# One mixing stage: two vector steps moved to GpSimd, value sums joined, the block solve's products spread over four column groups, and new turn orders

## The chip, the core and the metric

The program runs on one core of a Trainium2 chip. Five engines work side by side and meet only at semaphores: PE (TensorE, matrix products; PEld is its weight loading), DVE (VectorE), ACT (ScalarE), POOL (GpSimd) and SP (SyncE, which here only issues DMAs). The metric is the device time of one execution in microseconds (us), a median over several runs.

## The reference, cut to what matters

The program is one decoder layer on x of shape 32 x 128 x 256 (float32): a delta-rule attention, a cross attention and a mixture of experts, each followed by a layer norm. The change lies in the last part of the first of them, which for each head (H = 4, 64 values wide) and each row computes:

```python
T = inv(eye(32) - attn)                    # per chunk of 32 rows
u_i = u0 - w_i @ S ; o_i = q_i @ S + local @ u_i      # the delta rule, chunk by chunk
paths = stack([fir3(v), fir15(v), fir64(v), delta_path, v], axis=3)      # 5 paths of 64 per head
stats = mean, mean of squares, mean of |.|, norm of every path
logits = gelu(concat([hs, stats]) @ gW1 + gb1) @ gW2 + gb2
probs = softmax(logits / tau) * keep + eps
o = sum over paths of probs * paths
o = o * rsqrt(mean(o * o) + 1e-5) * norm_w
x = layernorm(x + o @ Wo)
```

The kernel solves the delta rule of a sequence of 128 rows as a triangular system of four blocks of 32 rows: each block's rows are a product of a matrix (`solver_blocks`) with the right side, in which the blocks solved before have been put in place.

## The kernel before

Everything happens in `mix_paths`. It works on pairs of sequences (P = 2, 16 pairs), 128 rows on the partitions. `staged_pair_loop` gives every engine a list of steps with a lag: in turn n of that engine's list, a step with lag k handles pair n - k. The list is the engine's program order, and an engine executes strictly in that order; between engines only the semaphores count. The first turns and the last ones are written out, the middle is a loop of two turns. A turn is one pass through a list.

What the steps do (lines of the kernel before):

- **PE**: `solve_rows(c)` (L1067), c = 0 to 3, forms block c of the solution: 8 products (2 sequences x 4 heads), each 128 rows x 32 columns of weights and 64 moving columns, all of one c into the same 32 PSUM partitions `rows` = 32c to 32c + 31, side by side in 512 columns. It waits for the block before to be copied back (`row_kept`). `scores` (L1033) makes the causal scores, `delta_rows` (L1079) the delta path, `cross_blocks` (L1047) the cross terms of the next pair, `hidden_x(0..3)` (L1103) and `hidden_stats(0..1)` (L1116) the gate's hidden layer, `logits` (L1126) its output, `statsT` (L1086) turns the statistics, `mixedT` (L1138) and `output` (L1146) turn the mix and multiply it by Wo.
- **ACT**: `keep_rows(c)` (L1183) copies block c from PSUM into `beta_r_v_to_solution`, one 32 x 512 copy, same partitions out as in. `keep_cross` (L1171, three copies), `norms` (L1199, a square root), `copy_stats` (L1206), `gelu(0..1)` (L1217), `exps` (L1226), `square_delta` (L1161), `square_paths` (L1191, L1193), `square_mix` (L1233), `copy_mixed` (L1240), `normalize` (L1246). Each of square root, gelu and exp is preceded by an ACT_TABLE_LOAD.
- **DVE**: `path_sums(t)` (L1289 over the filtered paths, L1290 over the values, sum and absolute sum for each of two sequences), `delta_sums` (L1297), `square_sums` (L1304), `mask_scores` (L1265), `shift_logits` (L1311 to L1321), `probabilities` (L1327 to L1337), `scale_delta` (L1276), `sum_paths` (L1347, and L1352 that adds the weighted delta path), `mix_norm` (L1357, L1360), `scale_mix` (L1366), `residual` (L1372 to L1385), `ln_shift` (L1392).
- **POOL**: `make_rhs` (L1411), `weight` (L1431, L1434), and two inverse roots, `mix_inverse` (L1441) and `ln_inverse` (L1449).
- **SP**: `load_solver`, `load_keys`, `load_gate`, `load_x`, `load_grams`, each waiting until its buffer's readers are done.

Waits that matter below: `cross_blocks` of a pair waits for `shift_logits` (semaphore `shifted`) of the pair two before it, since both use one PSUM bank; `scale_delta` waits until the pair two before it has had its delta path added (`mix_summed`), since both use one buffer; `square_mix` writes `residual`, which `normalize` of the pair before reads, so it waits for `x1_done`; `mix_norm` waits for `square_mix`.

## Time and profile before

| | us |
|---|---|
| median of 3 runs | 1570.22 |
| lowest and highest | 1565.67, 1572.8 |
| the profiled execution's own time | 1569.91 |
| its span, first to last instruction | 1568.2 |
| busy: PE, DVE, ACT, POOL | 1355.5, 915.1, 689.8, 541.7 |
| `mix_paths`, in that span | about 319 to 672 |

All sums below are made against the profiled execution (1569.91 us, of which 1568.2 is the span); the median lies 0.3 us above it. Of the rest of the program nothing is changed, so only the stretch of `mix_paths` is read: who is busy in a turn, who waits for whom, and how far apart the turns are. A row of the timeline merges like instructions: its start, its length to the end of the last of them, engine, line, names, shapes, count. Two neighbours on one engine often overlap by some 0.08 us, so what an instruction costs its engine is the distance to the next start, called its pace here. One product of float32 operands is recorded as two MATMULs, so 8 products are x16.

### The profile page before, as it was taken

Reading aid. Unit: us, or ns where it says so; the run is one execution under the profiler, and the core shown is the slowest. Engines: PE = TensorE matmul, PEld = TensorE weight load, DVE = VectorE, ACT = ScalarE, POOL = GpSimd, SP = SyncE. Lnnn points to the kernel's source line nnn. Section 1 sums busy time; section 2 is a strip of 40 time slices with the busy share of each in tenths; the row PEclk is TensorE's granted clock in tenths of the full one; section 3 lists DMA queues with packets and bytes.
Section 4 is the critical chain, followed back from the end, with each engine's and each line's share of the span. In section 5 each row is a group of like instructions: output and inputs, shape, how many; then the busy total and the mean of one; then the engine's idle time right before and its main releaser. Section 6 shows DMA issues by size and latency. Waiting matters only on the chain. (4 is left out here: it accounts for less than half of the span.)

```text
span 1568.2 us, 24828 instructions
## 1 busy us (share of the span) xinstructions
PE 1355.5 (86%) x8188; PEld 1035.6 (66%) x8189; DVE 915.1 (58%) x1735; ACT 689.8 (44%) x1253; POOL 541.7 (35%) x460
## 2 busy tenths in 40 slices
PE   4889556669999999569999999969979999999995
PEld 1344456658888888358888888855756666666653
DVE  4899759769999999535454445446512212122196
ACT  2545349947777777323433343331022222222214
POOL 2565500014555555522312331211234444444311
PEclk9999878889999999679999999979989999999998
DMA  3698787744333332042232021023021111111164
GB/s 89 149 244 234 207 221 198 216 121 104 95 94 94 94 94 61 14 123 71 85 98 98 31 62 61 28 81 110 0 74 54 57 57 55 56 56 57 59 200 134
DMA packets 147325, 158.20 MB, mean 101 GB/s; under 512 B 63440, under 2 KB 112176, under 8 KB 145712
## 3 DMA queue, kind: packets, MB, share of 16 engines
q1 hardware_dynamic: 134320, 123.63, 27.0%
q0 software_dynamic: 8320, 29.37, 7.3%
q10 hardware_dynamic: 4608, 4.20, 0.8%
q8 instruction: 46, 0.75, 0.2%
q14 instruction: 31, 0.25, 0.1%
HBM read 104.72 MB, written 42.99 MB: 94 GB/s over the span
## 5 line engine op out<-in xcount | busy, mean ns | idle before, releaser
L2531 DVE TENSOR_TENSOR hidden<-unit_psum,gate 128x352 f32<-128x352 f32 x72 | 37.8, 525 | 210.1 <-ACT gate L2494 210.1
L1944 POOL TENSOR_TENSOR scores<-scores,score_max 128x1024 f32<-128x1024 f32 x32 | 60.8, 1899 | 243.2 <-DVE score_max L1872 243.2
L478 PE MATMUL proj_psum<-filtered 128*128 128x512 f32 x192 | 96.0, 648 | 34.8 <-DMA filtered<-in_xT 28.1
L2462 PE MATMUL unit_psum<-wd,hiddenT 128*128 (+1 forms) x432 | 112.0, 395 | 14.2 <-issue 12.9
L549 PE MATMUL proj_psum<-window,toep 128*128 128x128 f32 x512 | 77.2, 319 | 46.8 <-DMA toep<-in_fir 24.3
L2393 POOL DMA_INDIRECT unit_rows<-x_rows,token_of_slot x72 | 69.8, 970 | 126.9 <-PE unit_psum L2436 104.4
L668 ACT ACTIVATE filtered<-proj_psum 32x512 f32<-32x512 f32 x168 | 98.6, 587 | 30.3 <-PE proj_psum L549 26.3
L549 PEld LDWEIGHTS proj_psum<-window,toep 128*128 128x128 f32 x512 | 73.4, 231 | 50.5 <-issue 47.6
L697 DVE SCALAR_TENSOR_TENSOR filtered<-proj_psum,conv_taps,filtered 128x508 f32<-128x508 f32 (+1 forms) x144 | 95.0, 733 | 19.3 <-ACT filtered L596 19.3
L2400 POOL DMA_INDIRECT outs<-unit_out,choice_of_slot x72 | 71.1, 987 | 99.8 <-DVE unit_out L2536 97.1
L2462 PEld LDWEIGHTS unit_psum<-wd,hiddenT 128*128 128x128 f32 (+1 forms) x432 | 76.4, 190 | 37.0 <-issue 29.1
L2445 PE MATMUL unit_psum<-wg,rowsT 128*128 x288 | 98.5, 465 | 0.6 <-ACT rowsT L2488 0.6
L2445 PE MATMUL unit_psum<-wu,rowsT 128*128 x288 | 98.1, 464 | 0.0
L2494 ACT ACTIVATE gate<-unit_psum 128x352 f32<-128x352 f32 x72 | 33.4, 463 | 132.1 <-PE unit_psum L2445 132.1
L478 PEld LDWEIGHTS proj_psum<-filtered 128*128 128x128 f32 x192 | 37.8, 207 | 77.9 <-issue 70.2
L2500 ACT ACTIVATE hiddenT<-unit_psum 128x256 f32<-128x256 f32 x72 | 27.6, 383 | 112.6 <-PE unit_psum L2453 112.6
L2445 PEld LDWEIGHTS unit_psum<-wu,rowsT 128*128 128x128 f32 x288 | 55.3, 192 | 31.1 <-issue 1.0
L1067 PEld LDWEIGHTS mix_psum<-beta_r_v_to_solution,solver_blocks 128*32 128x32 f32 x1024 | 59.4, 111 | 21.9 <-issue 16.0
L1067 PE MATMUL mix_psum<-beta_r_v_to_solution,solver_blocks 128*32 128x64 f32 x1024 | 69.7, 222 | 1.4 <-ACT beta_r_v_to_solution L1183 1.4
L2536 DVE COPY unit_out<-unit_psum 128x256 f32<-128x256 f32 x72 | 30.6, 424 | 67.6 <-PE unit_psum L2462 66.6
L1103 PE MATMUL mix_psum<-xT_tiles,gate_w_x 128*128 128x256 f32 x256 | 66.3, 392 | 0.0
L831 POOL TENSOR_TENSOR qk_ssq<-qk_ssq,minus_half 128x32 f32<-128x32 f32 x8 | 43.5, 5437 | 54.3 <-DVE qk_ssq L711 54.3
(286 smaller groups left out, 3258.5 us busy)
## 6 DMA issues: line engine op xcount, KB each, us to landing
toep<-in_fir SPq DMA_DIRECT2D x32, 384.0 KB, 4.0
neg_decay_blocks<-in_gw1s POOLq DMA_DIRECT2D x8, 1280.0 KB, 10.6
ndg<-filtered SPq DMA_DIRECT2D x8, 1024.0 KB, 6.1
neg_decay_gram<-ndg SPq DMA_DIRECT2D x16, 512.0 KB, 3.7
ctxT_tiles<-in_ctxT SPq DMA_DIRECT2D x16, 512.0 KB, 3.6
gathered<-outs SPq DMA_DIRECT2D x32, 256.0 KB, 3.0
window<-value SPq DMA_DIRECT2D x32, 192.0 KB, 4.0
filtered<-in_xT SPq DMA_DIRECT2D x8, 512.0 KB, 7.0
```

Source lines behind the costliest of these rows:

```text
L478: mm = pe.matmul(psum[:, pair_bank(n, p, m % 2), :], wqkv[m // KD][:, k, (m % KD) * 128:(m % KD) * 128 + 128], xT[:, u, k, :], start=(k == ...
L549: mm = pe.matmul(fir_psum[:, half_of(n), TC * w + c, :], toep[:, w, c, :], window[:, u, :, TC * w + c, :], start=True, stop=True)
L668: act.activation(out, kept, ACT.Copy).then_inc(kept_act[half_of(n)], 1)
L697: ins = dve.scalar_tensor_tensor(out=acc[:, :, s:L], in0=raw[:, :, 0:L - s], scalar=taps[:, c // KD, c % KD, TAPS - 1 - s:TAPS - s], in1=a ...
L831: pool.tensor_tensor(ssq[:, u, :, :], ssq[:, u, :, :], wide(wide(M.minus_half[:, 0], [128, 2 * H], 1), [128, BB, 2 * H], 1), ALU.pow).then ...
L1067: mm = pe.matmul(psum[rows, SOLVE, at:at + DV], solver[:, u, t, h, rows], xs[:, u, at:at + DV], start=True, stop=True)
L1103: mm = pe.matmul(psum[:, GATE + m // 2, at:at + P * L], gw1x[:, k, m * 128:m * 128 + 128], xT[:, k, :], start=(m % 2 == 0 and k == 0), sto ...
L1944: pool.tensor_tensor(sc[:, i % 2, t, :, :], sc[:, i % 2, t, :, :], wide(mx[:, t, :], [128, XH, L], 2), ALU.subtract).then_inc(shifted[t], 1)
L2393: pool.indirect_dma_start(out=rows[:, u, :], out_offset=None, in_=M.x2_dram[:, :], in_offset=bass.IndirectOffsetOnAxis(ap=M.token_of[:, n: ...
L2400: pool.indirect_dma_start(out=M.outs_dram[:, :], out_offset=bass.IndirectOffsetOnAxis(ap=M.choice_of[:, n:n + 1], axis=0), in_=done[:, u, ...
L2445: mm = pe.matmul(psum[:, u, bank, 0:EH], rowsT[:, u, k, :], w[:, bass.ds(chosen["gate_up"], 1), k, :].rearrange("p e n -> p (e n)"), start ...
L2462: mm = pe.matmul(psum[:, u, DOWN, 0:D], hidT[0:HR[t], u, t, :], M.wd[0:HR[t], bass.ds(chosen["down"], 1), t, :].rearrange("p e n -> p (e n)"),
```

## The change

1. `solve_rows(c)`: product (t, h) goes to PSUM partitions 32h to 32h + 31 (column group h of the array) and columns 64t on, instead of partitions 32c on and columns 256t + 64h on. `keep_rows(c)` becomes four copies of 32 x 128, one for each head, from partitions 32h on to partitions 32c on.
2. `path_sums` handles both sequences in one step: the value reductions are joined, 2 of 128 x 512 instead of 4 of 128 x 256. The 4 reductions over the filtered paths stay.
3. The addition of the delta path (`add_delta`) and `scale_mix` are issued by POOL instead of DVE.
4. All five lists have a new order, some lags are changed (POOL's `weight` 2 to 3, ACT's `exps` 1 to 2, SP's `load_x` 3 to 4), and two semaphores are added.

```diff
@@ sync @@
-            staged_pair_loop(sp, PAIRS, (load_solver, 1), (load_keys, 1), (load_gate, 1), (load_x, 3), (load_grams, 0))
+            staged_pair_loop(sp, PAIRS, (load_solver, 1), (load_x, 4), (load_keys, 1), (load_grams, 0), (load_gate, 1))
@@ tensor, solve_rows @@
-                            mm = pe.matmul(psum[rows, SOLVE, at:at + DV], solver[:, u, t, h, rows], xs[:, u, at:at + DV],
-                                           start=True, stop=True)
+                            mm = pe.matmul(psum[h * CB:h * CB + CB, SOLVE, t * DV:t * DV + DV], solver[:, u, t, h, rows],
+                                           xs[:, u, at:at + DV], start=True, stop=True)
@@ tensor, statsT @@
+                pe.wait_ge(path_sums_made, i + 1)
+                pe.wait_ge(delta_sums_made, i + 1)
@@ tensor @@
-            staged_pair_loop(pe, PAIRS, (solve_rows(0), 1), (hidden_x(2), 2), (hidden_x(3), 2), (solve_rows(1), 1),
-                             (mixedT, 4), (output, 4), (statsT, 2), (scores, 1), (hidden_stats(0), 2), (solve_rows(2), 1),
-                             (hidden_stats(1), 2), (solve_rows(3), 1), (logits, 2), (hidden_x(0), 1), (delta_rows, 1),
-                             (cross_blocks, 0), (hidden_x(1), 1))
+            staged_pair_loop(pe, PAIRS, (solve_rows(0), 1), (scores, 1), (hidden_x(0), 2), (hidden_x(2), 2),
+                             (solve_rows(1), 1), (hidden_x(3), 2), (mixedT, 4), (hidden_x(1), 2), (statsT, 2), (solve_rows(2), 1),
+                             (output, 4), (hidden_stats(0), 2), (hidden_stats(1), 2), (solve_rows(3), 1), (logits, 2), (delta_rows, 1),
+                             (cross_blocks, 0))
@@ scalar, keep_rows @@
-                    act.activation(xs[rows, u, :], psum[rows, SOLVE, :], ACT.Copy).then_inc(row_kept, 1)
+                    for h in range(H):
+                        a = act.activation(xs[rows, u, :].rearrange("p (b h d) -> p b h d", b=P, h=H)[:, :, h, :],
+                                           psum[h * CB:h * CB + CB, SOLVE, 0:P * DV].rearrange("p (b d) -> p b d", b=P), ACT.Copy)
+                    a.then_inc(row_kept, 1)
@@ scalar @@
-            staged_pair_loop(act, PAIRS, (square_delta, 1), (keep_cross, 0), (keep_rows(0), 0), (copy_mixed, 3), (norms, 1),
-                             (keep_rows(1), 0), (copy_stats, 1), (gelu(0), 1), (keep_rows(2), 0), (gelu(1), 1),
-                             (keep_rows(3), 0), (normalize, 3), (square_mix, 2), (exps, 1), (square_paths, 0))
+            staged_pair_loop(act, PAIRS, (exps, 2), (square_delta, 1), (keep_cross, 0), (keep_rows(0), 0), (norms, 1),
+                             (keep_rows(1), 0), (copy_mixed, 3), (copy_stats, 1), (keep_rows(2), 0), (gelu(0), 1), (gelu(1), 1),
+                             (keep_rows(3), 0), (square_paths, 0), (normalize, 3), (square_mix, 2))
@@ vector, path_sums @@
-                    for s, mag in ((0, False), (2, True)):
-                        dve.tensor_reduce(stat[:, u, t, 0:12, s], fir, AX.XY, ALU.add, apply_absolute_value=mag)
-                        dve.tensor_reduce(stat[:, u, t, 16:20, s], val, AX.XY, ALU.add, apply_absolute_value=mag)
+                for s, mag in ((0, False), (2, True)):
+                    for t in range(P):
+                        ins = dve.tensor_reduce(stat[:, u, t, 0:12, s], filtered_heads(M, tile(j, u, t)), AX.XY, ALU.add,
+                                                apply_absolute_value=mag)
+                    ins = dve.tensor_reduce(stat[:, u, :, 16:20, s], val, AX.X, ALU.add, apply_absolute_value=mag)
+                ins.then_inc(path_sums_made, 1)
@@ vector @@
-            staged_pair_loop(dve, PAIRS, (residual, 4), (sum_paths, 3), (ln_shift, 4), (mask_scores, 1), (path_sums(1), 0),
-                             (shift_logits, 2), (mix_norm, 3), (probabilities, 2), (scale_delta, 1), (scale_mix, 3),
-                             (delta_sums, 1), (square_sums, 1), (path_sums(0), 0))
+            staged_pair_loop(dve, PAIRS, (mask_scores, 1), (residual, 4), (sum_paths, 3), (ln_shift, 4),
+                             (shift_logits, 2), (scale_delta, 1), (mix_norm, 3), (delta_sums, 1), (probabilities, 2), (square_sums, 1),
+                             (path_sums, 0))
@@ gpsimd @@
+            def add_delta(j, u):
+                i = 2 * j + u
+                pool.wait_ge(mix_step, i + 1)
+                pool.tensor_tensor(mixed[:, :, :], mixed[:, :, :], delta[:, u, :, :], ALU.add).then_inc(mix_summed, 1)
+            def scale_mix(j, u):
+                i = 2 * j + u
+                pool.wait_ge(mix_power, i + 1)
+                own = mixed[:, :, :].rearrange("p b (h d) -> p (b h) d", d=DV)
+                pool.tensor_tensor(own, own, wide(mix_r[:, :], [128, P * H, DV], 2), ALU.mult).then_inc(mix_scaled, 1)
-            staged_pair_loop(pool, PAIRS, (ln_inverse, 4), (make_rhs, 0), (mix_inverse, 3), (weight, 2))
+            staged_pair_loop(pool, PAIRS, (make_rhs, 0), (weight, 3), (ln_inverse, 4), (add_delta, 3), (mix_inverse, 3),
+                             (scale_mix, 3))
```

The order of instructions at the places that the prediction speaks of, before and after. `path_squares` is written by the squaring steps, `value` by `normalize`, `residual<-mixed` by `square_mix`, `gate_exps` by `exps`, `gate_hiddenT` by `gelu`. ACT before, from the two gelus to the squares of the next pair:

```order
L1217 ACTIVATE gate_hiddenT<-mix_psum,gb 128x256 x2
L1183 ACTIVATE beta_r_v_to_solution<-mix_psum 32x512
L1217 ACTIVATE gate_hiddenT<-mix_psum,gb 128x256 x2
L1183 ACTIVATE beta_r_v_to_solution<-mix_psum 32x512
L1246 ACTIVATE value<-residual,ln_shift,ln_inverse_std 128x256 x2
L1233 ACTIVATE residual<-mixed 128x512
L1226 ACT_TABLE_LOAD
L1226 ACTIVATE gate_exps<-gate_logits 128x2x4x5
L1191 ACTIVATE path_squares<-filtered 128x768 x2
L1193 ACTIVATE path_squares<-value 128x2x256
```

ACT after, from the same gelus:

```order
L1224 ACTIVATE gate_hiddenT<-mix_psum,gb 128x256 x4
L1188 ACTIVATE beta_r_v_to_solution<-mix_psum 32x2x64 x4
L1198 ACTIVATE path_squares<-filtered 128x768 x2
L1200 ACTIVATE path_squares<-value 128x2x256
L1253 ACTIVATE value<-residual,ln_shift,ln_inverse_std 128x256 x2
L1240 ACTIVATE residual<-mixed 128x512
```

The squares of the paths now stand ahead of `normalize`, `exps` opens the next turn, and each copy of a block is four.

PE before, from `solve_rows(0)` on (32x64 is a product of the solve; the operand names are printed in the order moving, weights or the reverse):

```order
L1067 MATMUL mix_psum<-beta_r_v_to_solution,solver_blocks 32x64 x8
L1103 MATMUL mix_psum<-xT_tiles,gate_w_x 128x256 x4
L1067 MATMUL mix_psum<-beta_r_v_to_solution,solver_blocks 32x64 x8
L1138 MATMUL mix_psum<-ident,mixed 128x128 x4
L1146 MATMUL mix_psum<-wo,mixedT 128x256 x4
L1086 MATMUL mix_psum<-ident,path_stats 80x128 x2
L1033 MATMUL mix_psum<-qT_tiles,kT_tiles 128x128 x8
L1116 MATMUL mix_psum<-path_statsT,gw1s 128x256 x2
L1067 MATMUL mix_psum<-beta_r_v_to_solution,solver_blocks 32x64 x8
```

PE after, from `solve_rows(0)` on:

```order
L1069 MATMUL mix_psum<-beta_r_v_to_solution,solver_blocks 32x64 x8
L1035 MATMUL mix_psum<-qT_tiles,kT_tiles 128x128 x8
L1107 MATMUL mix_psum<-xT_tiles,gate_w_x 128x256 x4
L1069 MATMUL mix_psum<-beta_r_v_to_solution,solver_blocks 32x64 x8
L1107 MATMUL mix_psum<-xT_tiles,gate_w_x 128x256 x2
L1142 MATMUL mix_psum<-ident,mixed 128x128 x4
L1107 MATMUL mix_psum<-xT_tiles,gate_w_x 128x256 x2
L1090 MATMUL mix_psum<-ident,path_stats 80x128 x2
L1069 MATMUL mix_psum<-beta_r_v_to_solution,solver_blocks 32x64 x8
L1150 MATMUL mix_psum<-wo,mixedT 128x256 x4
L1120 MATMUL mix_psum<-path_statsT,gw1s 128x256 x4
```

Between `mixedT` and `output` there are now three other steps, and `output` stands ahead of the gate's second part, behind `solve_rows(2)`.

DVE after, from `sum_paths` to the sums of the delta path:

```order
L1355 TENSOR_REDUCE mixed<-filtered 128x256 x2
L1392 SCALAR_TENSOR_TENSOR ln_shift<-ln_mean_var,ln_inverse_std 128x2
L1319 TENSOR_TENSOR gate_logits<-mix_psum,gb 128x40
L1323 TENSOR_TENSOR gate_logits<-gate_logits,inv_tau 128x40
L1327 TENSOR_REDUCE gate_sums<-gate_logits 128x8
L1329 TENSOR_TENSOR gate_logits<-gate_logits,gate_sums 128x40
L1283 TENSOR_TENSOR delta_path<-mix_psum,rq 128x512
L1363 TENSOR_REDUCE mixed_mean_squares<-residual 128x8
L1366 TENSOR_SCALAR mixed_mean_squares<-mixed_mean_squares 128x8
L1304 TENSOR_REDUCE path_stats<-delta_path 128x2x4 x2
```

Before, `mask_scores` and four sums of `path_sums` stood between `ln_shift` and `shift_logits`; now they stand ahead of `residual`.

## Rows read from the trace of the kernel before

**Rows 1.** DVE timeline, starts of `square_sums`: start us, length us, engine, line, operation, names, shapes, count
```profile
341.59 2.81 DVE L1304 TENSOR_REDUCE path_stats<-path_squares 128x40 f32<-128x2560 f32 x1
...
396.15 2.81 DVE L1304 TENSOR_REDUCE path_stats<-path_squares 128x40 f32<-128x2560 f32 x1
...
612.59 2.80 DVE L1304 TENSOR_REDUCE path_stats<-path_squares 128x40 f32<-128x2560 f32 x1
```

**Rows 2.** DVE timeline, one turn in the middle of the stage
```profile
478.50 0.58 DVE L1290 TENSOR_REDUCE path_stats<-value 128x4 f32 x1
...
482.34 1.98 DVE L1347 TENSOR_REDUCE mixed<-filtered 128x256 f32 x2
...
485.01 0.15 DVE L1392 SCALAR_TENSOR_TENSOR ln_shift<-ln_mean_var,ln_inverse_std 128x2 f32<-128x2 f32 x1
...
488.93 0.18 DVE L1311 TENSOR_TENSOR gate_logits<-mix_psum,gb 128x40 f32<-128x40 f32 x1
...
489.62 0.20 DVE L1321 TENSOR_TENSOR gate_logits<-gate_logits,gate_sums 128x40 f32<-128x40 f32 x1
...
492.36 1.09 DVE L1366 TENSOR_TENSOR mixed<-mixed,mixed_inverse_norms 128x512 f32<-128x512 f32 x1
493.38 1.27 DVE L1297 TENSOR_REDUCE path_stats<-delta_path 128x8 f32<-128x512 f32 x2
```

**Rows 3.** PE timeline, one turn in the middle of the stage
```profile
473.71 1.99 PE L1103 MATMUL mix_psum<-xT_tiles,gate_w_x 128*128 128x256 f32 x8
475.63 1.08 PE L1067 MATMUL mix_psum<-beta_r_v_to_solution,solver_blocks 128*32 128x64 f32 x16
476.64 0.66 PE L1138 MATMUL mix_psum<-ident,mixed 128*128 128x128 f32 x4
478.06 1.99 PE L1146 MATMUL mix_psum<-wo,mixedT 128*128 128x256 f32 x8 [0.76 <-ACT mixedT L1240]
479.89 0.38 PE L1086 MATMUL mix_psum<-ident,path_stats 128*80 128x128 f32 x2
...
481.30 1.13 PE L1116 MATMUL mix_psum<-path_statsT,gw1s 80*128 80x256 f32 x4
...
489.96 1.57 PE L1047 MATMUL mix_psum<-inv_tiles,neg_decay_gram 128*96 128x96 f32 x16
```

**Rows 4.** PE timeline, earlier and later stages: products in column groups, and in row groups
```profile
45.18 1.92 PE L494 MATMUL proj_psum<-filtered,small_weights 128*32 128x512 f32 x12
...
878.78 1.17 PE L1675 MATMUL score_psum<-keyT,queryT 32*128 32x128 f32 x32
```

**Rows 5.** ACT timeline, copies of the filter stage, whose source and target quarters of the partitions differ
```profile
311.61 3.63 ACT L668 ACTIVATE filtered<-proj_psum 32x512 f32<-32x512 f32 x6
```

**Rows 6.** ACT timeline, one turn in the middle of the stage
```profile
482.47 0.84 ACT L1217 ACTIVATE gate_hiddenT<-mix_psum,gb 128x256 f32<-128x256 f32 x2 [0.39 <-PE mix_psum L1116]
...
486.16 1.44 ACT L1246 ACTIVATE value<-residual,ln_shift,ln_inverse_std 128x256 f32 x2
487.69 0.63 ACT L1233 ACTIVATE residual<-mixed 128x512 f32<-128x512 f32 x1
488.34 1.28 ACT L1226 ACT_TABLE_LOAD   x1
...
489.99 1.56 ACT L1191 ACTIVATE path_squares<-filtered 128x768 f32 x2
...
492.46 0.62 ACT L1161 ACTIVATE path_squares<-delta_path 128x512 f32<-128x512 f32 x1
493.10 0.90 ACT L1171 ACTIVATE solver_blocks<-mix_psum 32x256 f32<-32x256 f32 x3
```

**Rows 7.** POOL timeline, a 128 x 512 addition of `weight`
```profile
478.64 1.27 POOL L1434 TENSOR_TENSOR delta_path<-delta_path,own_weighted_value 128x512 f32<-128x512 f32 x1
```

**Rows 8.** DMA landings in two turns: target, queue, count, KB each, median us to landing
```profile
kT_tiles<-kT SPq DMA_DIRECT2D x2, 256.0 KB, 2.9
```

**Rows 9.** Busy us by engine in 20 us of the stage; then granted clock, DMA share, GB/s
```profile
core 0: us, PE busy (x) PEld busy (x) DVE busy (x) ACT busy (x) POOL busy (x), PEclk, DMA share, GB/s
460.00:480.00 20.00, 19.23 (x169) 16.09 (x168) 19.44 (x38) 15.40 (x26) 11.15 (x12) 1.00 0.33 92
```

26 lines of the change are left out of this document (10 added, 16 removed).

## The prediction

> **What bounds the kernel now.** I read the page first for the place of the stage, then the timeline of DVE over the whole stage for the length of a turn, then DVE, PE, ACT and POOL over one turn in its middle. The stage is periodic, so one start that recurs gives the turn: `square_sums` starts at 396.15 and, 11 turns on, at 612.59 [rows 1], so a turn lasts 216.44 / 11 = 19.68 us. Within it DVE has no wait on another engine at all; it goes from instruction to instruction. PE looks as full (19.23 us busy in 20, DVE 19.44 [rows 9]), but two rows show that it follows: `output` starts after 0.76 us of waiting for the copy that PE's own `mixedT` feeds [rows 3], and `cross_blocks` starts at 489.96, 0.14 us behind the end of `shift_logits` (489.62 + 0.20) [rows 2, 3]. So DVE sets the turn at 19.68 us, and PE alone would need at most 19.68 us, 18.92 of it work. The two are nearly balanced: DVE relieved alone gives little, and PE relieved alone gives nothing.
>
> **What leaves DVE.** The addition: from the end of the two reductions one instruction is gone. They take 1.98 from 482.34, and the next could start 0.08 before their end, at 484.24; `ln_shift` started at 485.01 [rows 2]. That is 0.77 us. `scale_mix`: 492.36 to 493.38 [rows 2], 1.02 us. The value sums: one of 256 elements takes 0.58, a pace of 0.50 after the overlap [rows 2]. The trace has no joined one. If the cost is a fixed part of 0.06 plus one that grows with the elements, two of 512 cost 2 x (2 x 0.44 + 0.06) = 1.88 against 4 x 0.50 = 2.00, 0.12 less; if a joined one cost no more per element than the delta path's (512 elements, 1.27 for two, [rows 2], some 0.64), the four became 1.28, 0.72 less; if order or strides hurt, up to nothing less. I take 0.12, since the value's stride stays what it is. DVE's own work becomes 19.68 - 0.77 - 1.02 - 0.12 = 17.77 us a turn.
>
> **What DVE's new order adds.** In the new order `mix_norm` stands close behind `ln_shift`. Between them ACT must do `normalize` (which needs `ln_shift`), then `square_mix` (which overwrites what `normalize` reads), and only then may `mix_norm` read. From the start of `ln_shift`: 0.15, then about 0.04 to ACT, 1.53 to the start of `square_mix` (486.16 to 487.69), 0.63, and 0.03 back [rows 2, 6], together 2.38 us. DVE has in that time 0.07, `shift_logits` 0.81 (488.93 to 489.62, 0.20, less the overlap) and `scale_delta` about 0.65, some 1.53. So it waits 0.8 us, and its turn is 17.77 + 0.8 = 18.6. `scale_delta` itself now waits for POOL's `add_delta`: 1.27 by the like addition [rows 7], against 0.9 us of DVE's work, a wait inside the 0.8 and no extra. What queues behind this wait on DVE is everything up to `square_sums`. POOL has the room: its two new steps cost 1.3 each, 11.15 us busy in 20 [rows 9]; `weight` still ends ahead of `sum_paths`, and `scale_mix` ends over 1 us before PE comes to `mixedT`.
>
> **The solve on PE.** A round of 16 MATMULs now has a pace of 1.01 (475.63 to 476.64), (1.08 - 0.22) / 15 = 0.057 from one start to the next, 0.22 being the length of one [rows 3]. Nothing in this stage has four column groups. The nearest row is L494: three column groups, 128 x 32 weights, 512 moving columns, 12 in 1.92 us [rows 4]. Its length of one is 0.59, so the starts lie 0.12 apart; eight times the columns of the solve at the solve's own pace would be 0.46 apart. Products in different column groups do run beside each other. How closely short ones can follow is bounded by L1675, in four row groups: (1.17 - 0.27) / 31 = 0.029 [rows 4]. That gives 15 x 0.029 + 0.22 = 0.66, less the overlap 0.07: about 0.60 a round. The bounds are 0.40 (each group keeps its own pace, four deep) and 1.01 (no gain). I take S = 0.60, as L1675 is the fastest stream in this trace.
>
> The Trainium skill (TensorE: Matmul & The Clock Gate, part 3, "The mechanism") says that weight loads overlap with running products only when the row group differs; all products here use all rows, and by that S would stay 1.01. The same page gives a gain for three column groups at 512 columns. L494 speaks for the second: its starts are 0.12 apart and each start needs its own weight load. The rule is the third rival below.
>
> **The copies on ACT.** Four copies of 32 x 128 take the place of one of 32 x 512 with 0.59. Three copies of 256 elements take 0.90 [rows 6], one 0.36 with an overlap of 0.09; one of 512 in the filter stage takes 0.59. So an element costs 0.23 / 256 and a copy of 128 about 0.25. Whether they overlap is the question: those of the filter stage, whose quarters of the partitions differ as they will here, do not (6 in 3.63, 0.605 each) [rows 5]. I take K = 4 x 0.25 + 3 x 0.02 = 1.05 a block. Bounds: 0.72 with the overlap, 4 x 0.36 = 1.45 if a copy has the price of one of 256 elements.
>
> **The loop through ACT and PE.** This is where those two prices count. Follow the new lists from one `normalize` to the next; all from [rows 3, 6]: `normalize` 1.53, `square_mix` 0.65, the exp table and `exps` 1.58 (1.28 + 0.28 and a gap), `square_delta` 0.64, `keep_cross` 0.81, copy of block 0 K; to PE 0.1, `solve_rows(1)` S, `hidden_x(3)` 0.96 (half of 1.92), `mixedT` 0.60, `hidden_x(1)` 0.96, `statsT` 0.32, `solve_rows(2)` S, `output` 1.83, both `hidden_stats` 2 x 1.06, `gelu(1)` 0.84 and 0.06 to reach ACT, copy of block 3 K, `square_paths` 2.47 (489.99 to 492.46). The fixed parts are 15.5, so the loop is 15.5 + 2K + 2S = 15.5 + 2.1 + 1.2 = 18.8 us. It is a little longer than DVE's 18.6, so it sets the turn: **18.8 us**. PE's own work is 18.92 - 4 x 0.41 = 17.3, and the 0.76 of waiting before `output` is covered by `hidden_x(1)`, `statsT` and `solve_rows(2)` (1.9 us against 1.4). PE then waits about 1.5 us a turn, in pieces.
>
> **The new waits and SP.** `statsT` waits for two more semaphores; both are given before `square_sums` ends, which `norms` needs anyway: nothing. On SP `load_x` stands ahead of `load_keys` and waits for the `residual` of its turn; the keys are then issued some 4 to 5 us ahead of `scores`, and landing took 2.9 [rows 8]. Nothing, but the cover is only 1 to 2 us.
>
> **The sum.** Eleven full turns gain 19.68 - 18.8 = 0.88 each: 9.7. The first three intervals, 341.59 to 396.15, were 54.6 us [rows 1], and hold less work in every list: solve and copies count there (PE ran them without DVE), and the last of them, 20.5, becomes a plain turn. I put their gain at 1.4, 1.6 and 1.7: 4.7. The first pair, with four rounds in a row (each 0.4 less on PE, 0.45 more on ACT, with fewer steps between), gains 1.0, the last interval 1.0. Emptying the stage costs 1.5 more, since `output` (1.99) now runs ahead of the gate's second part there with no solve to fill. Together 9.7 + 4.7 + 1.0 + 1.0 - 1.5 = 14.9. From 1569.91: **1555 us**.
>
> **Rivals.**
> (a) Both halves better: copies overlap (K = 0.72) and S = 0.40 makes the loop 17.8; the DVE wait holds the turn at 18.6, or 18.0 if the value sums are cheap as well. 11 x 0.2 to 11 x 0.8 more: 1546 to 1552. For it: the copies within `keep_cross` do overlap. Against: rows 5.
> (b) Copies at the price of 256 elements (K = 1.45): the loop is 19.6, the eleven turns gain 1, and the rest about 4: 1565. For it: nothing shows that ACT is cheaper below 256 elements out of PSUM.
> (c) The solve gains nothing (S = 1.01), by the rule cited: the loop is 15.5 + 2.1 + 2.0 = 19.6, again about 1565. Against it: L494. Half way on either, 1558 to 1562.
> (d) Slower: the copies. If each costs as a 32 x 512 one does in the filter stage, that is, if the time of such a copy were mostly fixed, K = 4 x 0.6 = 2.4, the loop is 21.5 and 11 x 1.8 = 20 us are lost, 4 gained at the ends: about 1585. The point from which it decides is K = 1.5 at S = 0.60 (15.5 + 2K + 1.2 = 19.68). For it: nothing but that no copy of this size is in the trace; against it three of 256 elements in 0.90.
> (e) The change does not do what it says, because another resource holds the turn at 19.7 (POOL late for `sum_paths`, keys late): 1566 to 1572.
>
> **Chances.** The forecast, turns of 18.5 to 19.1 (1551 to 1559): 0.52. (a) 0.12. (b) and (c) with the half ways: 0.20, two fifths of that below 1562. (e) 0.07. (d) and any other loss 0.09. A measurement of this kernel tells about 0.5% from no change, 7.9 us. Faster by more (below 1562.4): 0.52 + 0.12 + 0.08 = 0.72; within: 0.12 + 0.07 = 0.19; slower: 0.09. The range from 1547 to 1567 leaves out most of (d), half of (e) and the lower part of (a), under 0.2.
>
> **What would show it.** Starts of `square_sums` 18.8 apart instead of 19.68. On DVE a wait of 0.5 to 1 us ahead of `mix_norm`, released by `square_mix`, and none elsewhere; `normalize` starting directly behind `square_paths` with no wait on `ln_shift` if the ACT loop decides, and with one if DVE's does. The solve as 16 MATMULs in about 0.66, the four copies in about 1.05. No wait of PE before `output`. Wrong would be: a turn set by a wait of DVE on POOL, a copy of over 0.36, a wait of PE on keys, or a fall of the granted clock, which is 1.00, its upper level of 2.4 GHz, in the middle of the stage [rows 9] and which more idle PE time could lower.

## The result and the profile after

The changed kernel took 1587.22 us (median of 4 runs, 1586.04 to 1589.53), the kernel before 1571.51 in the same comparison: a ratio of 1.011 with an interval of 1.0089 to 1.0131. It is slower by 1.1%, where 1555 had been forecast. The profiled run had 1586.04 us, a span of 1584.1 and a granted clock of 0.906 over the whole program, against 1569.91, 1568.2 and 0.937 before.

The 16.5 us that the stage ends later come from its pieces, read from the starts of `square_sums` and the ends of the stage:

| piece | before | after | difference |
|---|---|---|---|
| start of the stage (nothing before it was changed) | 318.99 | 321.94 | +2.95 |
| from there to the first `square_sums` | 22.60 | 22.98 | +0.4 |
| the first three intervals | 54.6 | 62.6 | +8.0 |
| eleven turns | 216.4 | 218.3 | +1.8 |
| the last interval | 18.4 | 20.1 | +1.7 |
| emptying | 41.0 | 42.6 | +1.6 |

The first line is scatter of the work ahead of the stage: over the profiles of all twenty kernels here the stage begins between 314.8 and 322.0. The forecast had gains of 1.0, 4.7, 9.7 and 1.0 on the second to the fifth line and a loss of 1.5 on the last. The first three intervals miss it by 12.7 and the eleven turns, at 19.84 us each, by 11.5. With the other lines that makes the 31 us between the forecast and the profiled 1586.04.

DVE timeline of the kernel after, the starts that answer to [rows 1]:

```profile
344.92 2.81 DVE L1312 TENSOR_REDUCE path_stats<-path_squares 128x40 f32<-128x2560 f32 x1
...
407.52 2.81 DVE L1312 TENSOR_REDUCE path_stats<-path_squares 128x40 f32<-128x2560 f32 x1
...
625.80 2.81 DVE L1312 TENSOR_REDUCE path_stats<-path_squares 128x40 f32<-128x2560 f32 x1
```

Busy us by engine in the same 20 us as [rows 9], with the same columns (the granted clock is the third number from the end):

```profile
460.00:480.00 20.00, 18.99 (x171) 16.32 (x170) 19.49 (x33) 17.31 (x38) 12.86 (x13) 0.84 0.37 103
```

Two things stand here that the forecast did not have. DVE is as busy as before (19.49 against 19.44) though it has given up 1.9 us of work a turn. Over the eleven turns its waits come to only 3.6 us, so 19.52 of the 19.84 us of a turn are its own instructions, where 17.77 had been forecast. And the clock is 0.84, a mixture of its two levels, 1.2 and 2.4 GHz, where it was 1.00.

**Where DVE's gain went.** DVE and POOL timelines of the kernel after, one turn:

```profile
460.78 0.15 DVE L1392 SCALAR_TENSOR_TENSOR ln_shift<-ln_mean_var,ln_inverse_std 128x2 f32<-128x2 f32 x1
460.85 0.19 DVE L1319 TENSOR_TENSOR gate_logits<-mix_psum,gb 128x40 f32<-128x40 f32 x1
461.08 1.20 DVE L1323 TENSOR_TENSOR gate_logits<-gate_logits,inv_tau 128x40 f32<-128x40 f32 x1
...
465.99 0.20 DVE L1342 TENSOR_TENSOR gate_exps<-gate_exps,gate_sums 128x40 f32<-128x40 f32 x1
466.23 0.95 DVE L1345 TENSOR_TENSOR gate_exps<-gate_exps,floor 128x40 f32<-128x40 f32 x1
467.11 2.81 DVE L1312 TENSOR_REDUCE path_stats<-path_squares 128x40 f32<-128x2560 f32 x1
...
471.56 1.04 DVE L1297 TENSOR_REDUCE path_stats<-value 128x8 f32 x1
```
```profile
460.94 1.27 POOL L1439 TENSOR_TENSOR mixed<-mixed,delta_path 128x512 f32<-128x512 f32 x1 [1.29 <-DVE mixed L1355]
...
466.01 1.08 POOL L1445 TENSOR_TENSOR mixed<-mixed,mixed_inverse_norms 128x512 f32<-128x512 f32 x1
```

L1323 works on 40 elements, as L1342 does in 0.20, but is booked with 1.20: it ends at 462.28, when POOL's `add_delta` ends (462.21). L1345 is booked with 0.95 and ends at 467.18, POOL's `scale_mix` at 467.09. So 1.0 + 0.7 us of the time moved to POOL stands on DVE again, as long instructions and not as waits; no view of waits names them. Both are DVE instructions with two inputs in SBUF. L1319, with one of its inputs in PSUM, ran over the start of the addition in its 0.19. The two lengthenings, 1.00 and 0.72, are the difference between 19.52 and 17.77.

The Trainium skill (SBUF — State Buffer, "SBUF: two separate sides") has the rule: VectorE and GpSimd share a pair of ports, and a VectorE instruction with two SBUF inputs and a GpSimd instruction that reads SBUF exclude each other for whole instructions. The trace agrees for POOL's two steps of 128 x 512, with 1.20 against 0.20. It does not for POOL's inverse root on 8 elements: DVE's L1334 has two inputs in SBUF as well and takes its 0.20 in the middle of one. Here the measurement decides; these runs don't settle which of POOL's instructions block. POOL and then DVE timeline of the kernel before:

```profile
490.70 1.63 POOL L1441 TENSOR_TENSOR mixed_inverse_norms<-mixed_mean_squares,minus_half 128x8 f32<-128x8 f32 x1 [6.16 <-DVE mixed_mean_squares L1360]
```
```profile
491.22 0.20 DVE L1334 TENSOR_TENSOR gate_exps<-gate_exps,gate_sums 128x40 f32<-128x40 f32 x1
```

The blocking could have been seen in the trace of before. There POOL's product for `own_weighted_value`, which now takes 0.76, took 1.21 beside DVE's `scale_mix`, and that `scale_mix` took 1.09 [rows 2] where it takes 0.69 at the end of the stage, with POOL idle. So 0.4 of the 1.02 us that DVE was to give up with it was blocking already. POOL and then DVE timeline of the kernel before:

```profile
492.87 1.21 POOL L1431 TENSOR_TENSOR own_weighted_value<-value,gate_exps 128x256 f32<-128x256 f32 x1
```
```profile
661.26 0.69 DVE L1366 TENSOR_TENSOR mixed<-mixed,mixed_inverse_norms 128x512 f32<-128x512 f32 x1 [1.75 <-POOL mixed_inverse_norms L1441]
```

**What the clock took.** PE timeline of the kernel after, from the last solve round of a pair:

```profile
456.28 0.43 PE L1069 MATMUL mix_psum<-beta_r_v_to_solution,solver_blocks 128*32 128x64 f32 x16
457.28 1.96 PE L1130 MATMUL mix_psum<-gw,gate_hiddenT 128*128 128x20 f32 x16 [0.57 <-ACT gate_hiddenT L1224]
459.09 3.35 PE L1081 MATMUL mix_psum<-beta_r_v_to_solution,causal_scores 128*128 128x64 f32 x16
462.88 2.85 PE L1049 MATMUL mix_psum<-inv_tiles,neg_decay_gram 128*96 128x96 f32 x16 [0.44 <-DVE gate_logits L1329]
465.66 0.66 PE L1069 MATMUL mix_psum<-beta_r_v_to_solution,solver_blocks 128*32 128x64 f32 x16
```

`cross_blocks` was 1.57 in [rows 3] and is 2.85, `delta_rows` was 1.89 and is 3.35: this turn runs two products at the lower level for most of their length, 2.7 us more. `cross_blocks` is that long in every turn of the middle; `delta_rows` varies from 1.98 to 3.58. Ahead of the fall PE did a short solve round (0.43), waited 0.57 and did the 16 products of 20 columns of `logits`.

### The profile page after: what moved, and what is told of

It reads as the page before. It is cut to its first block and busy times, and to the rows that moved or that the text cites. A ratio compares the mean times of both kernels' runs of the same rounds, so it can differ in the third digit from the quotient of the medians.

```text
span 1584.1 us, 24989 instructions
## 1 busy us (share of the span) xinstructions
PE 1355.2 (86%) x8188; PEld 1038.4 (66%) x8189; DVE 909.0 (57%) x1671; ACT 721.1 (46%) x1445; POOL 573.4 (36%) x492
## 5 line engine op out<-in xcount | busy, mean ns | idle before, releaser
L697 DVE SCALAR_TENSOR_TENSOR filtered<-proj_psum,conv_taps,filtered 128x508 f32<-128x508 f32 (+1 forms) x144 | 95.0, 733 | 18.5 <-ACT filtered L596 18.5
L1188 ACT ACTIVATE beta_r_v_to_solution<-mix_psum 32x128 f32<-32x128 f32 x256 | 68.6, 268 | 6.9 <-PE mix_psum L1069 3.5
L1049 PE MATMUL mix_psum<-inv_tiles,neg_decay_gram 128*96 128x96 f32 x256 | 45.5, 372 | 22.5 <-DMA inv_tiles<-inv 14.7
```

The source lines that it names most:

```text
L697: ins = dve.scalar_tensor_tensor(out=acc[:, :, s:L], in0=raw[:, :, 0:L - s], scalar=taps[:, c // KD, c % KD, TAPS - 1 - s:TAPS - s], in1=a ...
L1049: mm = pe.matmul(psum[0:L - CB, CROSS + t, at:at + L - CB], nd[:, t, h, 0:L - CB], inv[:, t, h, CB:L], start=True, stop=True)
L1188: a = act.activation(xs[rows, u, :].rearrange("p (b h d) -> p b h d", b=P, h=H)[:, :, h, :], psum[h * CB:h * CB + CB, SOLVE, 0:P * DV].rea ...
```

## The experiments

All were compared with the kernel before in the same call. The clock is that of the stretch from 400 to 600 us, the turn is from the starts of `square_sums` there. The kernel before had medians of 1568.8 to 1573.2 in these comparisons, so where two rows are compared below, each is first set against its own.

| kernel | median us | ratio to before | clock | turn us |
|---|---|---|---|---|
| after | 1587.2 | 1.011 [1.0089, 1.0131] | 0.84 | 19.84 |
| e1 before + column groups | 1614.5 | 1.0284 [1.023, 1.0338] | 0.81 | 22.3 |
| e2 before + both steps on POOL | 1566.9 | 0.9989 [0.9966, 1.0013] | 1.00 | 19.57 |
| e3 after, solve as before | 1590.8 | 1.0136 [1.0091, 1.018] | 0.91 | 19.4 / 21.7 |
| e4 after, both steps on DVE | 1599.0 | 1.0178 [1.0125, 1.0231] | 0.83 | 21.2 |
| e5 after, collisions hidden | 1593.2 | 1.0142 [1.0103, 1.0181] | 0.83 | 20.1 to 20.9 |
| e6 after, denser PE order | 1594.9 | 1.0142 [1.0107, 1.0177] | 0.90 | 19.4 to 21.4 |
| e7 after + filler | 1575.9 | 1.0034 [1.0012, 1.0055] | 0.92 | 19.4 to 20.8 |
| e8 e5 and e6 together | 1597.2 | 1.015 [1.0108, 1.0193] | 0.87 | 19.5 / 20.9 |
| e9 e5 + filler in two places | 1579.4 | 1.0063 [1.0038, 1.0088] | 0.94 | 18.95 to 20.95 |
| e10 e1 + filler | 1572.6 | 1.0027 [1.0009, 1.0045] | 1.00 | 19.70 |
| e11 e1 and e2 + filler | 1555.0 | 0.9908 [0.9879, 0.9937] | 1.00 | 18.82 |
| e12 e2, output later | 1615.9 | 1.0308 [1.0281, 1.0336] | 0.94 | 21.9 to 23.5 |
| e13 e11 without filler | 1607.8 | 1.0219 [1.0182, 1.0256] | 0.81 | 22.3 |
| e14 before + filler | 1580.0 | 1.005 [1.0033, 1.0067] | 1.00 | 20.46 |
| e15 e11 + joined sums | 1560.7 | 0.9922 [0.9897, 0.9947] | 1.00 | 18.84 |
| e16 e1, products twice | 1588.9 | 1.0105 [1.0068, 1.0141] | 0.91 | 19.7 / 21.4 |
| e17 e11, half the filler | 1585.4 | 1.0106 [1.0086, 1.0126] | 0.91 | 18.8 and 22.3 |
| e18 e11, filler elsewhere | 1631.1 | 1.0401 [1.0379, 1.0424] | 0.78 | 24.0 |

**One part at a time.** e1 has the column groups and the copies by head alone, e2 the two steps on POOL alone, in the old lists. The first diff is the solve in e1 (its copies are those of the change), the second is POOL's list in e2 (the two steps are gone from DVE).

```diff
-                            mm = pe.matmul(psum[rows, SOLVE, at:at + DV], solver[:, u, t, h, rows], xs[:, u, at:at + DV],
-                                           start=True, stop=True)
+                            mm = pe.matmul(psum[h * CB:h * CB + CB, SOLVE, t * DV:t * DV + DV], solver[:, u, t, h, rows],
+                                           xs[:, u, at:at + DV], start=True, stop=True)
```

```diff
-            staged_pair_loop(pool, PAIRS, (ln_inverse, 4), (make_rhs, 0), (mix_inverse, 3), (weight, 2))
+            staged_pair_loop(pool, PAIRS, (ln_inverse, 4), (add_delta, 3), (make_rhs, 0), (mix_inverse, 3),
+                             (scale_mix, 3), (weight, 2))
```

> The kernel before with one part of the change alone: the solve in four column groups and its rows copied in four copies a block; all lists, POOL's work and the value sums as before. Theory (two causes: the shared access of DVE and POOL, and the clock): DVE still sets the turn, so DVE's work stays 19.7 us a turn and the time stays within 0.5% as long as the clock holds; a round of 16 in 0.43 us, four copies in 1.10. If the compressed rounds alone lower the granted clock (rival: the column groups are the cause of the clock), the middle of the stage shows about 0.85 instead of 1.00 and the kernel comes out at 1578 to 1590. If the order of the products is the cause, the clock stays 1.00 and the time 1568 to 1576.

> The kernel before with the addition and the scaling on POOL instead of DVE, everything else in the old order. Theory: DVE's small steps with two SBUF inputs that meet a POOL step wait until it ends, as L1323 (1.20 instead of 0.20) and L1345 (0.95 instead of 0.23) do in the changed kernel. What meets what here: the addition runs while DVE does mask_scores and reductions, the scaling while DVE does the sums of the delta path or the probabilities. So DVE's turn falls from 19.7 to between 18.0 and 18.7, and PE, which alone needs up to 19.5, sets the turn: 1563 to 1571. Rival (POOL blocks DVE wherever it works): no gain on DVE, 1570 and more.

e1: the column groups, meant to shorten PE's work, alone lower the clock to 0.81 and cost 45 us. `delta_rows` takes 3.5 and `cross_blocks` 2.7 to 2.8 in every turn of that stretch. e2: with the old lists the moved steps meet no DVE instruction with two SBUF inputs (the addition runs beside `mask_scores`, which reads PSUM and takes 1.21 as before); DVE is busy 180.98 of 200 us (before 194.59) and has 1.2 us of waiting for `output` in each turn. The turn is 19.57 all the same: PE sets it now, and a tenth of a us a turn is all that DVE's relief gives.

**The parts undone, and both causes met by order.** e3 and e4 take one part out of the changed kernel. e5 gives the POOL steps other company on DVE; e6 moves PE work between `logits` and `cross_blocks`; e8 is both.

In DVE's list, e5:

```diff
-(mask_scores, 1), (residual, 4), (sum_paths, 3), (ln_shift, 4), (shift_logits, 2),
+(residual, 4), (sum_paths, 3), (ln_shift, 4), (mask_scores, 1), (shift_logits, 2),
...
-(probabilities, 2), (square_sums, 1),
+(square_sums, 1), (probabilities, 2),
```

In PE's list, e6 (the two `hidden_x` are those that the change has at lag 2 ahead of `statsT`):

```diff
-(logits, 2), (delta_rows, 1), (cross_blocks, 0)
+(logits, 2), (hidden_x(0), 1), (delta_rows, 1), (hidden_x(1), 1), (cross_blocks, 0)
```

> The changed kernel with the solve undone: all products of a round in one column group, one copy of 32x512 a block. Theory (the order of the products, sparse ones behind each other, lowers the clock): the clock stays near 0.85 and PE, with 0.6 us more a round, is slower still: 1590 to 1610. Rival (the column groups lower the clock): it returns to 1.00, delta_rows and cross_blocks to 1.8 and 1.4 us, and the turn to 19.6: 1565 to 1580.

> The changed kernel with the addition and the scaling back on DVE (scaling behind the sums of the delta path), new lists otherwise. Theory: DVE's two small steps return to 0.20 and 0.23 us (1.7 us less), the two moved ones cost 1.4 to 1.8, so DVE's turn is the same within 0.3 us and the time within 0.5% of the changed kernel (1580 to 1593). Rival (the steps on POOL are a gain that the clock hides): 1.8 us a turn slower, about 1605 to 1615.

> The changed kernel with two steps of DVE's list in other places: mask_scores behind ln_shift, so that it (one SBUF input) and not L1323 runs beside POOL's addition, and square_sums ahead of the probabilities, so that it runs beside POOL's scaling. Theory: the two collisions (1.00 and 0.72 us a turn) are gone, DVE's work falls from 19.5 to about 17.9 a turn. What is late next is PE at its lower clock (about 18.3 busy of 20 and waits of 1.1 a turn that are replies to DVE and ACT): turns of 18.8 to 19.5, 1572 to 1582, the clock still near 0.84. Rival (the clock alone sets the turn): no change, 1583 to 1592.

> The changed kernel with PE's list changed: hidden_x(0) and (1) of the next pair stand around delta_rows again, ahead of cross_blocks, as before. Theory: logits, delta_rows and cross_blocks are no longer one stretch, but the compressed rounds remain, so the clock rises only in part (0.84 to 0.88..0.95); DVE still has its collisions, 19.4 to 19.6: 1578 to 1587. Rival (the order is the whole cause of the clock): 1.00, and turns of 19.4, 1568 to 1575.

> The changed kernel with both edits, DVE's two steps in other places and PE's denser list. Theory: if both causes count, this gains more than either: turns of 18.6 to 19.2, 1562 to 1574, limited by what is left of the lower clock. Rival (one of them is no cause): the same as the better of the two single edits within 3 us.

e3: with the old solve the clock still falls, to 0.91, so the new order of PE does it too. e4: DVE pays 1.24 for its own scaling (0.69 where POOL is idle) and waits 0.56 for POOL's inverse; its turn becomes 21.2, and the clock is 0.83. e5: the collisions are gone, and nothing is won. DVE and then PE timeline of e5:

```profile
459.28 0.20 DVE L1323 TENSOR_TENSOR gate_logits<-gate_logits,inv_tau 128x40 f32<-128x40 f32 x1
...
462.31 0.69 DVE L1283 TENSOR_TENSOR delta_path<-mix_psum,rq 128x512 f32<-128x512 f32 x1 [2.37 <-PE mix_psum L1081]
```
```profile
459.29 2.88 PE L1081 MATMUL mix_psum<-beta_r_v_to_solution,causal_scores 128*128 128x64 f32 x16 [0.80 <-DVE causal_scores L1272]
```

DVE's L1323 is 0.20, and its busy time fell to 169.69 of 200 (kernel after 192.05), but `delta_rows` now waits for the `mask_scores` that was moved back, and DVE waits 2.4 us for a `delta_rows` that runs mostly at the lower level. e6: the order is denser ahead of `cross_blocks` and thinner ahead of `statsT`, which now waits 1.10 for `norms`, and ahead of a solve round that waits 0.65. In seven of eleven turns `cross_blocks` is 1.52 long, at the upper level, but in three of these `output`, behind the new waits, takes 3.4 to 3.6 where [rows 3] have 1.99; in the other four the fall is where it was (`delta_rows` 3.5, `cross_blocks` 2.8). So the fall moved in part. e8 has both orders and is no better than either.

**Work that nobody reads.** If the clock falls because PE does too little at that place, adding work there must make the kernel faster. e7 is the changed kernel with

```diff
 def logits(j, u):
+    for _ in range(4):
+        pe.matmul(psum[:, CROSS, 384:512], gw1x[:, 0, 0:128], M.wo[:, 0, 0:128], start=True, stop=True)
     pe.wait_ge(gelu_done, 2 * (i + 1))
```

> The changed kernel with four more products (128x128 weights, 128 moving columns, about 0.9 us) ahead of logits, into PSUM columns that nobody reads; nothing else. They fill the wait of 0.57 for the gelu. Theory (PE's idle and sparse stretch from solve_rows(3) to cross_blocks lowers the clock): more work makes PE faster; the clock rises above 0.90 in the middle of the stage and delta_rows goes back from 3.0 to 1.9 us; DVE's collisions hold the turn at 19.4 to 19.6, 1575 to 1583. Rival (more work is only more work): PE gets 0.3 to 0.9 us longer a turn, 1590 to 1600.

> The changed kernel with both causes met in another way than in the run with both orders undone: VectorE's collisions hidden (mask_scores behind ln_shift, square_sums ahead of probabilities, as in the run with the collisions hidden), and four products of 128 x 128 by 128 columns, which nobody reads, ahead of logits and four more ahead of delta_rows (they add work and leave the output alone). Theory (the two causes are the collisions and TensorE's clock): with neither, VectorE is busy 17.0 us of a turn and TensorE is at the level of 2.4 GHz most of the stage, delta_rows back at about 1.9; the turn falls under the 19.45 that the single filler showed, to 18.5 to 19.0, and the kernel to 1560 to 1570. Rival (the wait of delta_rows for mask_scores, 0.8 us, is a third cost of this order of VectorE and sets the turn): the clock recovers, but the turn stays at 19.4 or above and the kernel at 1573 to 1580. Rival (eight products cost more than they give): the turn is at 20 or more, TensorE's busy time grows by 2.3 us a turn and the kernel is at 1585 or more.

PE timeline of e7:

```profile
464.53 1.16 PE L1128 MATMUL mix_psum<-wo,gate_w_x 128*128 128x128 f32 x8
465.52 1.86 PE L1132 MATMUL mix_psum<-gw,gate_hiddenT 128*128 128x20 f32 x16
467.23 1.98 PE L1081 MATMUL mix_psum<-beta_r_v_to_solution,causal_scores 128*128 128x64 f32 x16
```

The filler costs 1.0 us of PE's time (464.53 to 465.52) and stands where PE had waited 0.57. `delta_rows` is back at 1.98, and the kernel is 11 us faster than the changed one. Most of that is won at the start of the stage, where the clock is 0.91 from 340 to 400 instead of 0.77: the first three intervals take 55.9 us instead of 62.6. The eleven turns are 19.74 each against 19.84. The collisions are still there (1.19 and 0.95) and keep the turn from going under 19.4. Nor is the fall all gone: `cross_blocks`, which now waits up to 1.66 for the `shift_logits` that contains the blocked L1323, is 2.8 long in seven of the eleven turns. e9, with four filler products ahead of `logits` and four ahead of `delta_rows`, has no collisions, but it is not rid of the fall (0.94, with three of ten stretches of 20 us at 0.83), nor of the wait that the new DVE order brought (1.47 us and more before `scale_delta`, for a `delta_rows` that waits for `mask_scores`): turns of 19 to 21 where the theory had 18.5 to 19.0. The changed orders don't get to the forecast turn by these means, and no run here shows that they can.

**The same test on the kernel before.** So the old lists, which have no collision, were taken: e10 is e1 with the filler, e11 is e1 and e2 together with the filler, e13 is e11 without it, e14 is the kernel before with nothing but the filler.

> The kernel before with the column groups and the copies by head alone, as in the run of the column groups alone (1614.5, granted clock 0.81), and four products of 128 x 128 by 128 columns that nobody reads ahead of logits (they add work and leave the output alone). Theory (the 43 us of that run are the clock's, not the copies'): the granted clock goes back to 0.9 or more, turns to 20 to 20.5, and the kernel to 1575 to 1590; what is left above the kernel before is the dearer copies (4 x 0.66 us) less the shorter solve (4 x 0.58) and the 0.6 of the filler. Rival (the copies and the waits for them in the old orders made the 43 us, and the clock followed the waits): the filler gives less than 10 us, the kernel stays at 1605 or more.

> The kernel before with both steps on POOL (as in the run of POOL's steps alone: 1566.9, turn 19.57, no collisions), the column groups with the copies by head, and the four products that nobody reads ahead of logits (they add work and leave the output alone); all the orders but the places of the two steps are those of before. TensorE sets the turn of 19.57 there. Theory (the solve's products are worth having where the clock holds): its chain is shorter by 4 x 0.58 us of products and longer by 4 x 0.66 of copies and 0.6 to 1.2 of filler, so the turn is 20 to 20.5 and the kernel 1572 to 1585, clock 0.9 or more. Rival (with the old orders the copies run beside other TensorE work and cost nothing): turn 18.5 to 19, kernel 1555 to 1563, faster than both. Rival (the clock falls in spite of the filler, since VectorE no longer sets the pace and TensorE waits for copies): clock under 0.87, kernel at 1595 or more.

> The kernel of 1555.0 us (the kernel before, both steps on POOL, column groups with copies by head, old orders, filler) without its filler. Theory (TensorE's time sets the turn there only because the clock is held): the filler's 0.6 to 1.2 us a turn goes, and the granted clock of the stage falls with it, from 1.00 to 0.85 or lower, turns to 21 or more; the kernel is at 1595 to 1615, like the run of the column groups alone. Rival (VectorE's shorter chain alone had made the difference to the run of the column groups alone, and the filler is dead weight here): clock 0.95 or more, turns of 18.2 to 18.8, kernel 1545 to 1555.

> The kernel before with nothing but the four products that nobody reads ahead of logits (they add work and leave the output alone). Its stage is already at a granted clock of 1.00. Theory (the filler gives only what the clock had lost): nothing to win in the stage; VectorE sets the turn with TensorE close behind, so its 0.6 to 1.2 us of TensorE time cost 0 to 1.0 us a turn: kernel 1568 to 1584, no run of turns under 19.6. Rival (the filler helps otherwise, by holding TensorE's sequence in step with the others): turns under 19.5, kernel at 1563 or less.

e10 against e1 is 42 us, e11 against e13 is 48 us, from four products that nobody reads. e14 is the control: where the clock is 1.00 already, the same products cost 7 us, and the turn is 20.46, near the 19.57 of e2 plus 1.0; PE's own chain needs that. So the gain of e10 and e11 comes with the clock (0.81 to 1.00) and not from the products as such. The rows of PE around that place, in e13 and then in e11:

```profile
459.90 0.43 PE L1067 MATMUL mix_psum<-beta_r_v_to_solution,solver_blocks 128*32 128x64 f32 x16 [0.64 <-ACT beta_r_v_to_solution L1184]
460.77 2.28 PE L1126 MATMUL mix_psum<-gw,gate_hiddenT 128*128 128x20 f32 x16 [0.43 <-ACT gate_hiddenT L1220]
462.88 2.05 PE L1103 MATMUL mix_psum<-xT_tiles,gate_w_x 128*128 128x256 f32 x4
464.73 3.51 PE L1079 MATMUL mix_psum<-beta_r_v_to_solution,causal_scores 128*128 128x64 f32 x16
```
```profile
460.91 0.43 PE L1067 MATMUL mix_psum<-beta_r_v_to_solution,solver_blocks 128*32 128x64 f32 x16 [0.64 <-ACT beta_r_v_to_solution L1186]
461.27 1.16 PE L1124 MATMUL mix_psum<-wo,gate_w_x 128*128 128x128 f32 x8
462.26 1.86 PE L1128 MATMUL mix_psum<-gw,gate_hiddenT 128*128 128x20 f32 x16
463.97 1.11 PE L1103 MATMUL mix_psum<-xT_tiles,gate_w_x 128*128 128x256 f32 x4
464.91 1.89 PE L1079 MATMUL mix_psum<-beta_r_v_to_solution,causal_scores 128*128 128x64 f32 x16
```

The products from L1103 and L1079 are the same ones, 2.05 against 1.11 and 3.51 against 1.89. From 400 to 600 PE is busy for 183.91 us in e13 and 183.93 in e11, at clocks of 0.81 and 1.00. e11 is also the version that beats both kernels: 1555.0 us, 0.9% under the kernel before and 2% under the changed one. The theory had its turn at 20 to 20.5, and its first rival was right: of the 2.6 us by which the dearer copies were to lengthen the chain, the waits of PE for them show 0.64 and 0.17. e10 has turns of 19.70 with DVE busy 194.67 of 200 us, as before: without e2, DVE sets the turn and the shorter solve is worth nothing. Each half gives nothing alone (e2 0.9989, e10 1.0027); together, at a full clock, they give 0.9%.

**What is left open, narrowed.** e12 moves `output` behind `statsT` and `scores` in e2 (`(mixedT, 4), (statsT, 2), (scores, 1), (output, 4)`), e15 joins the value sums in e11, e16 issues each of e1's solve products twice, e17 has two filler products instead of four, e18 has the four ahead of `statsT` instead of ahead of `logits`.

> The kernel before with both steps on POOL (1566.9, turn 19.57, VectorE idle 1.2 us a turn in front of the residual, TensorE idle 0.76 ahead of output for the copy of mixedT), and output moved behind statsT and scores in TensorE's list; solve and copies as before. Theory (TensorE sets that turn by its work and its waits): 0.7 us of the wait goes, the turn is 18.9, and the kernel 1556 to 1562, faster than the kernel before. Rival (another wait takes its place: statsT then waits for norms, or VectorE gets output later than it wants it): turn 19.4 to 19.8, kernel 1564 to 1570. Rival (the order brings TensorE's clock down, as both other orders did): clock under 0.95, turn 20 or more, kernel 1575 or more.

> The kernel of 1555.0 us (before, both steps on POOL, column groups with copies by head, old orders, filler) with the value sums of the two tiles joined in one reduction each, as the changed kernel has them; in that run VectorE waits 0.2 us a turn and TensorE 0.8 for the copy of mixedT. Theory (TensorE's chain with its waits sets the turn of 18.82, VectorE has 0.2 of slack): the 0.12 to 0.2 us that VectorE wins become idle time; the kernel stays within 3 us of 1555. Rival (VectorE sets it and TensorE's waits are its slack): turn 18.65 to 18.7, kernel 1551 to 1553.

> The kernel before with the column groups and the copies by head alone (1614.5, clock 0.81), with each of the solve's products issued twice to the same place with the same result (added work, the output alone is as before): 32 products a round, about 0.79 us, so that TensorE is busy in the solve nearly as long as with the old products (1.01). Theory A (the clock follows the share of time in which TensorE is busy): the clock goes back to 0.95 or more, turns to 20 to 20.5, kernel 1575 to 1590. Theory B (products that use only a quarter of the columns of the array at a time count for less in what the clock follows, whatever their number): the clock stays at 0.80 to 0.87, and the kernel at 1605 to 1625, its turns at 22 or more.

> The kernel of 1555.0 us (before, both steps on POOL, column groups with copies by head, old orders, filler) with two filler products instead of four (they add work that nobody reads). Without any it is 1607.8, at a granted clock of 0.81 in the stage. Theory A (there the clock is full or not, and two suffice): clock 0.98 or more, the turn shorter by the 0.5 us of two products or where VectorE's 18.6 stop it, 18.6 to 18.8, kernel 1551 to 1556. Theory B (two are too little work in that place): clock 0.81 to 0.92, turns of 19.5 to 22, kernel 1570 to 1605.

> The kernel of 1555.0 us with its four filler products ahead of statsT, right behind output, instead of ahead of logits; no wait stands there, so they fill none and add 1 us of work some 4 us earlier in the turn (nobody reads them). Theory A (what counts is work in the stretch before logits, where the solve's last two rounds wait for copies): the clock falls all the same, 0.81 to 0.92, kernel at 1580 to 1612. Theory B (what counts is the work of a turn, wherever it stands): clock 0.98 or more, kernel 1553 to 1562.

e12 was to save PE a wait of 0.76. It made one of 2.3 instead (`statsT` now comes before `norms` is done), and behind that wait the clock falls. The larger part of the 47 us is waiting: DVE now waits 3.7 to 5.4 us a turn for `output`, against 1.2 in e2. PE timeline of e12:

```profile
470.83 0.42 PE L1086 MATMUL mix_psum<-ident,path_stats 128*80 128x128 f32 x2 [2.27 <-ACT path_stats L1196]
471.17 1.23 PE L1033 MATMUL mix_psum<-qT_tiles,kT_tiles 64*128 64x128 f32 x16
472.33 3.57 PE L1146 MATMUL mix_psum<-wo,mixedT 128*128 128x256 f32 x8
```

e15: no gain; the intervals of e11 and e15 overlap and the mean turn is 18.84 against 18.82. DVE does not set the turn of e11. Nor does PE's work, since e17's good turns, with half the filler, are 18.86 as well. What remains is the loop from PE's `mixedT` and solve rounds through ACT's copies and back, but no run took a copy away, so this stays a guess.

e16: 32 products in 0.69 in place of 16 in 0.43 bring half of the clock back (0.91) and 30 us. Neither reading of its forecast holds alone. e17 shows two regimes in one execution. The rows are its stretches of 20 us from 440 on (columns as in [rows 9]):

```profile
440.00:460.00 20.00, 17.74 (x174) 14.22 (x173) 18.85 (x35) 18.27 (x43) 14.13 (x15) 1.00 0.34 93
460.00:480.00 20.00, 18.37 (x163) 15.66 (x164) 17.97 (x35) 16.61 (x35) 13.95 (x16) 0.83 0.33 92
480.00:500.00 20.00, 18.60 (x145) 15.81 (x145) 15.34 (x34) 16.36 (x34) 11.49 (x12) 0.80 0.33 92
```

Its turns are 18.8 to 18.9 us long from 402 to 458, then for six turns 19.4 to 22.4, and 18.8 again at the end, with the same instructions in the same order. The busy share of PE doesn't tell the two apart: it is 17.74 of 20 at the full clock and 18.60 at 0.80, since the slower products are booked for longer. e18 shows that the place matters more than the amount: the same four products, 1.05 us, put behind `output`, where no wait stands, leave the clock at 0.78 and the turn at 24.0, longer than without them. PE timeline of e18:

```profile
464.05 0.43 PE L1067 MATMUL mix_psum<-beta_r_v_to_solution,solver_blocks 128*32 128x64 f32 x16 [0.63 <-ACT beta_r_v_to_solution L1186]
464.91 3.02 PE L1128 MATMUL mix_psum<-gw,gate_hiddenT 128*128 128x20 f32 x16 [0.43 <-ACT gate_hiddenT L1222]
```

So in the old lists the fall is tied to the thin place between the solve's last rounds and `logits`: two short rounds, waits of 0.63 and 0.43, then products of 20 columns. Open is how the three weigh against each other. In other lists it also comes elsewhere, as behind the waits in e6 and e12.

## Why the prediction was wrong, point by point

Two steps of the sum failed. DVE's own work was to fall to 17.77 us a turn and stayed at 19.52, since two of its instructions stood still beside POOL's new ones. And the loop through ACT and PE left out a wait for DVE and took PE's clock for granted: it fell from 1.00 to 0.84, which cost most in the first intervals of the stage.

- **What bounds the kernel** (DVE at 19.68, PE close behind it): right. e2 relieves DVE and gets 19.57; e14 loads PE with 1.0 more and gets 20.46.
- **What leaves DVE** (0.77 + 1.02 + 0.12): right as to instructions. The joined value sum is 1.04 long with a pace of 0.96, two for 1.92, as forecast within 0.04. Wrong was the step "DVE's own work becomes 17.77": it is 19.52, since the two steps stayed on DVE as 1.7 us of blocking. This is the first step that failed, and it alone keeps every turn at 19.4 or more. "POOL has the room" looked at POOL's busy time and not at what DVE would run beside it. The list of what would be wrong named a DVE wait on POOL; what came was no wait in the trace but a longer instruction. It is a mechanism that no rival had.
- **The wait in DVE's new order** (0.8 before `mix_norm`): in 7 of 11 turns there is one, 3.6 us in all, up to 0.75. In the turn shown it is not there, since the blocked L1323 ahead of it takes up the time.
- **S**, forecast 0.60: a pace of 0.36 (16 MATMULs in 0.43). The bound of 0.40 below was too high, since starts 0.014 apart ((0.43 - 0.22) / 15) are closer than in the fastest stream of the trace before (0.029). Rival (c) took from the Trainium skill (TensorE: Matmul & The Clock Gate, Part 3, "The mechanism") that weight loads overlap only where the row group differs. By that the pace would have stayed 1.01; the row of 0.43 above does not agree, and the measurement decides.
- **K**, forecast 1.05: right. ACT timeline of the kernel after:

```profile
457.25 1.10 ACT L1188 ACTIVATE beta_r_v_to_solution<-mix_psum 32x128 f32<-32x128 f32 x4
```

- **The loop through ACT and PE**, 18.8: this is the second step that failed. Its terms left out two things. First, ACT's `norms` stands between the copy of block 0 and `statsT`, and it waits for DVE's `square_sums`, 0.92 to 1.36 us in every turn, so the chain that recurs runs through DVE: `mix_norm`, `square_sums`, `norms`, the gate, `normalize`, `square_mix` and back. From 423.78 to 443.91 it took 20.13 us, 0.72 of them the blocked L1345, and 1.18 of them waits of ACT for PE. DVE and ACT timelines of the kernel after:

```profile
423.78 0.69 DVE L1363 TENSOR_REDUCE mixed_mean_squares<-residual 128x8 f32<-128x512 f32 x1 [0.75 <-ACT residual L1240]
...
443.91 0.69 DVE L1363 TENSOR_REDUCE mixed_mean_squares<-residual 128x8 f32<-128x512 f32 x1 [0.47 <-ACT residual L1240]
```
```profile
430.42 0.28 ACT L1206 ACTIVATE path_stats<-path_stats 128x40 f32<-128x40 f32 x1 [1.36 <-DVE path_stats L1312]
```

  Second, `delta_rows` and `cross_blocks` are in no term of the loop, yet PE has to do them ahead of what ACT waits for, and at a clock of 0.84 they are some 2 us a turn longer together, at most 3.0. How much of the 1.18 us is theirs no run shows. The prediction named a fall of the clock as a way to be wrong, and gave it neither a price nor a chance. It took its own "PE then waits about 1.5 us a turn, in pieces" as harmless, and the change took 2.6 us of work (4 x 0.65) out of a PE that ran at the full clock with 0.76 of waiting.
- **The first three intervals**, forecast 4.7 less: 8.0 more. In the stretches from 340 to 400 the clock is 0.76, 0.76 and 0.81, where all three had 1.00 before, and the filler of e7 wins 6.7 us back there. So most of the 8.0 us is the clock's. The shorter solve, which was to count there at once, is in part what lowered it: e1, with the new solve and its copies alone, has 0.76, 0.76 and 0.84 in the same stretches.
- **`statsT`, `load_x`, no wait before `output`, and 1.5 us for the emptying** (measured 1.6): right.
- **Rival (d)**, the one on the slower side, had dear copies; they cost what was forecast. The slower side came from other causes.

The figure of 18.8 us a turn was reached in the end, by e11, with the old lists and work that nobody reads. That the two figures agree is chance: e11 does not run the loop that was summed.

## What to carry to other kernels

Where PE runs at the full clock with small products and little waiting, count work taken away from it as a risk: look at the granted clock by stretches, and at the thinnest place of the turn, and test with a few products that nobody reads at that place before giving up a shorter chain. Before moving an elementwise step from DVE to POOL, list what DVE will run beside it: instructions with a PSUM input and most reductions ran beside it undisturbed here (a value sum took 0.67 instead of 0.58 beside `make_rhs`), and those with two SBUF inputs stood still until POOL's 128 x 512 steps had ended. When two engines bound a turn, relief of one shows nothing; try the two reliefs together before judging either.

## What the runs showed of the hardware

- Sixteen products of 128 x 32 weights and 64 columns in four column groups take 0.43 us against 1.08 in one (a pace of 0.36 against 1.01), though all use all rows. The copies of 32 x 128 from PSUM take 0.27 each on ACT and don't overlap (four in 1.10).
- The clock can fall in a stage where PE is busy for over 90% of the time, and four products more or less at one place decided 48 us of 1600. In e17 both regimes alternate within one execution.
- A DVE instruction that is blocked by POOL is shown as a long one and not as idle time: 40 elements in 1.20 us. Beside POOL's inverse root on 8 elements a like instruction took its 0.20.
